# Two attention layers and a mixture of experts on one core: layer normalisations on ScalarE, their factors on GpSimd, GroupNorm's scale from PSUM, and new orders for all engines

## The reference, cut to what matters

```python
# layer 1: GroupNorm (16 groups of 4 channels), full attention, residual
h = group_norm(x, gn_scale, gn_bias, 16)
q, k, v = h@wq + bq, h@wk + bk, h@wv + bv
x = x + softmax(q k^T / 8) v @ wo + bo
# layer 2: LayerNorm over 64 channels, causal attention, residual
n = (t - mean(t)) / sqrt(var(t) + 1e-5)
t = t + softmax(mask((n Wq^T)(n Wk^T)^T / 8)) (n Wv^T)
# layer 3: LayerNorm, then 32 experts that each choose 8 tokens of an image
u = (t - mean(t)) / sqrt(var(t) + 1e-5)
probs = softmax(u gate_w^T + gate_b, over tokens)
vals, idx = top_k(probs, 8)
out = t + scatter_add(idx, vals * expert(sum(vals * u[idx])))
```

## Time and profile before

| | |
|---|---|
| median of 3 runs | 1007.56 us |
| the profiled execution: its own time | 1003.97 us |
| its span, first to last instruction | 1001.9 us |
| TensorE (PE) busy | 844.6 us, 84% |
| VectorE (DVE) busy | 718.1 us, 72% |
| ScalarE (ACT) busy | 409.4 us, 41% |
| GpSimd (POOL) busy | 348.1 us, 35% |
| granted TensorE clock, mean over the span | 0.921 |

### The profile page before, as it was taken

How to read it: one execution, slowest core, us unless ns; L and a number is a source line. 1 busy time by engine, 2 the same in 40 slices (tenths; PEclk the granted TensorE clock), 3 DMA queues, 4 the chain that set the end, 5 groups by cost and what they waited for, 6 DMA issues and landing times. The chain is left out here.

```text
span 1001.9 us, 14825 instructions
## 1 busy us (share of the span) xinstructions
PE 844.6 (84%) x4406; PEld 486.5 (49%) x4406; DVE 718.1 (72%) x1853; ACT 409.4 (41%) x792; POOL 348.1 (35%) x182
## 2 busy tenths in 40 slices
...
DMA packets 63017, 30.70 MB, mean 31 GB/s; under 512 B 35279, under 2 KB 60271, under 8 KB 62959
## 3 DMA queue, kind: packets, MB, share of 16 engines
...
...
## 5 line engine op out<-in xcount | busy, mean ns | idle before, releaser
L967 DVE TENSOR_REDUCE neg_max<-maxima_in 128x1 f32<-128x1024 f32 (+7 forms) x256 | 253.3, 990 | 106.1 <-PE maxima_in L654 93.6
L819 ACT ACTIVATE probs<-scores 128x512 f32<-128x512 f32 (+3 forms) x464 | 233.7, 538 | 163.2 <-PE scores L681 158.2
L876 POOL TENSOR_TENSOR prob_sum<-prob_sum,probs 128x1024 f32<-128x1024 f32 x96 | 227.3, 2368 | 117.3 <-ACT probs L819 112.4
L654 PE MATMUL maxima_in<-keys,queries 128*128 128x512 f32 (+3 forms) x496 | 175.2, 427 | 22.6 <-DVE neg_max L967 19.1
L681 PE MATMUL scores<-queries,keys 128*128 128x512 f32 (+3 forms) x464 | 177.0, 382 | 0.0
L696 PE MATMUL values_out<-probs,x_sb 128*64 128x512 f32 x512 | 138.1, 636 | 0.0
L654 PEld LDWEIGHTS maxima_in<-keys,queries 128*128 128x128 f32 x496 | 90.4, 207 | 88.8 <-DVE neg_max L967 58.6
L876 POOL TENSOR_TENSOR prob_sum<-probs 128x1024 f32<-128x1024 f32 x16 | 38.1, 2384 | 238.4 <-ACT probs L819 238.4
L855 POOL TENSOR_TENSOR ln<-ln,minus_half 128x8 f32<-128x8 f32 x32 | 52.7, 1648 | 192.0 <-DVE ln L1004 190.5
L679 PE MATMUL scores<-queries_lo,keys_hi 65*128 65x512 f32 x256 | 115.4, 451 | 2.3 <-DMA queries_lo<-max_rows 2.3
L681 PEld LDWEIGHTS scores<-queries,keys 128*128 128x128 f32 x464 | 91.6, 197 | 8.0
...
## 6 DMA issues: line engine op xcount, KB each, us to landing
...
```

What stands on the lines that cost most here:

```text
L654: mm = pe.matmul(maxima_in[:, lo:lo + w * P], weights, keys[s][q][:, h * HALF:h * HALF + w * P], start=not diagonal, stop=True, skip_group ...
L819: nc.scalar.activation(of(probs[:, t % NP, :]), shape(scores[:, bank_of(s, u), 0:w]), ACT.Exp, scale=SCALE).then_inc(exp_done, 1)
L876: nc.gpsimd.tensor_tensor(prob_sum[:, :], before, probs[:, t % NP, :], ALU.add).then_inc(rows_added, 1)
L967: V.tensor_reduce(neg_max[s][:, at:at + 1], maxima_in[:, HALF - widths[0] * P:HALF + widths[1] * P], AX.X, ALU.max, negate=True).then_inc( ...
```

## The change

It does four things.

1. The normalisations `l1n` and `l2n` go from VectorE to ScalarE, as factor x t + bias with factor and bias from a column each. For that, `l1p` and `l2p` on GpSimd become four operations of 128 x 8 instead of one: variance + epsilon (`ve`, before on VectorE), mean x -1 (`ng`), the power (`rs`), and -mean x factor (`nm`).
2. GroupNorm: `d` reads the group means straight from PSUM and makes difference and square in two operations that both read PSUM; `g2` averages only the square; `ab` becomes two operations on ScalarE.
3. `w_scaled` is made by a step of its own on ScalarE, `ws`, and `out1` waits for it.
4. All engines' lists are written anew. `out2`, `ri2` and `f2` come at the end of the turn before (`@-1`), `p1.tr` becomes `@+2`, at the end of a turn, and `xb` becomes `@+1`.

The core of the diff:

```diff
 ORDER = {
...
-    "pool": "ad.1 ad.2 pw@+1 ad.3 l2p@-2 ad.4 ad.5 ad.6 ad.7 xb l1p",
-    "sp": "st@-2 su@-2 row2@-1 xload@+2 row1@+1 sl@-2",
+    "pool": "l2p@-2 ad.1 ad.2 pw@+1 ad.3 ad.4 ad.5 ad.6 ad.7 xb@+1 l1p",
+    "sp": "su@-2 st@-2 sl@-2 row2@-1 xload@+2 row1@+1",
...
             elif name == "g2":
-                pe.wait_ge(gn_step, done("gn_step", n, "d2"))
-                pe.matmul(fin_ps[:, 0:2], group_mean[:, :], gn[:, 4:6], start=True, stop=True).then_inc(fin_step, 1)
+                pe.matmul(fin_ps[:, 0:1], group_mean[:, :], gn[:, 5:6], start=True, stop=True).then_inc(fin_step, 1)
...
                 if s == 1:
-                    pe.wait_ge(fin_step, done("fin_step", "w", n, "wb"))
+                    pe.wait_ge(weights_scaled, done("weights_scaled", "ws", n, "ws"))
...
+            elif name == "ab":
+                act.wait_ge(gn_step, done("gn_step", n, "pw"))
+                nc.scalar.activation(affine[q][:, 0:1], gn[:, 7:8], ACT.Identity, bias=0.0,
+                                     scale=const("gn_scale")).then_inc(gn_step, 1)
+                act.wait_ge(gn_step, done("gn_step", n, "a"))
+                nc.scalar.activation(affine[q][:, 1:2], affine[q][:, 0:1], ACT.Identity, bias=const("gn_bias"),
+                                     scale=gn[:, 2:3]).then_inc(gn_step, 1)
+            elif name == "ws":
...
+                nc.scalar.activation(w_scaled[q][:, :], w_out[1][:, :], ACT.Copy, scale=affine[q][:, 0:1]).then_inc(
+                    weights_scaled, 1)
+            elif name in ("l1n", "l2n"):
...
+                act.wait_ge(norm_step[s], done(f"norm{s}_step", n, "nm"))
+                for t in range(NT):
+                    ins = nc.scalar.activation(dst[:, t, 0:width], src[:, t, 0:width], ACT.Identity, bias=ln[s][:, 0, t:t + 1],
+                                               scale=ln[s][:, 1, t:t + 1])
+                ins.then_inc(norm_step[s], 1)
...
             elif name in ("l1p", "l2p"):
                 s = int(name[1])
+                pool.wait_ge(norm_step[s], done(f"norm{s}_step", n, "ag"))
+                nc.gpsimd.tensor_tensor(ln[s][:, 0, :], ln_mv[s][:, :, 1], eps_ln[:, :], ALU.add).then_inc(norm_step[s], 1)
+                nc.gpsimd.tensor_tensor(ln[s][:, 2, :], ln_mv[s][:, :, 0], minus_one[:, :], ALU.mult).then_inc(norm_step[s], 1)
                 pool.wait_ge(norm_step[s], done(f"norm{s}_step", n, "ve"))
                 nc.gpsimd.tensor_tensor(ln[s][:, 1, :], ln[s][:, 0, :], minus_half[:, :], ALU.pow).then_inc(norm_step[s], 1)
+                pool.wait_ge(norm_step[s], done(f"norm{s}_step", n, "rs"))
+                nc.gpsimd.tensor_tensor(ln[s][:, 0, :], ln[s][:, 2, :], ln[s][:, 1, :], ALU.mult).then_inc(norm_step[s], 1)
...
             elif name == "d":
                 dve.wait_ge(fin_step, done("fin_step", "g1", n, "mm"))
-                V.tensor_copy(gn[:, 2:4], fin_ps[:, 0:2]).then_inc(fin_step, 1)
-                dve.wait_ge(fin_step, done("fin_step", "g1", n, "gv"))
-                V.tensor_scalar(gn[:, 4:6], gn[:, 0:2], gn[:, 2:3], None, ALU.subtract).then_inc(gn_step, 1)
+                V.tensor_scalar(gn[:, 2:4], fin_ps[:, 0:2], -1.0, None, ALU.mult).then_inc(fin_step, 1)
+                V.tensor_scalar(gn[:, 4:5], fin_ps[:, 0:1], gn[:, 0:1], None, ALU.subtract).then_inc(gn_step, 1)
                 dve.wait_ge(gn_step, done("gn_step", n, "d"))
-                V.tensor_tensor(gn[:, 4:6], gn[:, 4:6], gn[:, 4:6], ALU.mult).then_inc(gn_step, 1)
+                V.scalar_tensor_tensor(out=gn[:, 5:6], in0=fin_ps[:, 0:1], scalar=gn[:, 0:1], in1=gn[:, 4:5],
+                                       op0=ALU.subtract, op1=ALU.mult).then_inc(fin_step, 1)
...
-            elif name == "ab":
...
-                V.tensor_scalar(w_scaled[q][:, :], w_out[1][:, :], affine[q][:, 0:1], None, ALU.mult)
...
-                dve.wait_ge(norm_step[s], done(f"norm{s}_step", n, "ag"))
-                V.tensor_scalar(ln[s][:, 0, :], ln_mv[s][:, :, 1], EPS_LN, None, ALU.add).then_inc(norm_step[s], 1)
-            elif name in ("l1n", "l2n"):
...
```

More of the change, by code:

```diff
@@ L91 @@
 OWN_STEPS["pe"].update({f"v{s}.{t}": (f"values_done{s}", ["v"]) for s in (1, 2) for t in range(NT)})
[L93 to L94 removed]
+IN_TURN = {"gn_step": ["ag", "d", "pw", "a", "b", "wh", "wl"],
+           "norm1_step": ["bn", "ag", "ve", "ng", "rs", "nm", "v"], "norm2_step": ["bn", "ag", "ve", "ng", "rs", "nm", "v"]}
 FIRST_TURN, LAST_TURN = -2, B + 2
@@ L345, in attention_part @@
     ln_mv = {s: sb(f"ln_mv{s}", [P, NT, 2]) for s in (1, 2)}
-    ln = {s: sb(f"ln{s}", [P, 2, NT]) for s in (1, 2)}
+    ln = {s: sb(f"ln{s}", [P, 3, NT]) for s in (1, 2)}
     x_stack = sb("x_stack", [P, S], F32R)
@@ L375, in attention_part @@
     ones_f = sb("ones_f", [P, P])
-    minus_half = sb("minus_half", [P, NT])
+    minus_half, minus_one, eps_ln = (sb(name, [P, NT]) for name in ("minus_half", "minus_one", "eps_ln"))
     group_mean = masks_f[:, 0, :]
@@ L752, in run @@
                 nc.scalar.copy(keys[2][q][0:C, HALF:S], proj_ps[C:P, :]).then_inc(proj_step, 1)
+            elif name == "ab":
[6 more added lines that the diff above has]
+            elif name == "ws":
+                act.wait_ge(gn_step, done("gn_step", n, "a"))
+                if exists(n + (-2)):
+                    act.wait_ge(fin_step, done("fin_step", "out1", n + (-2), "mm"))
+                nc.scalar.activation(w_scaled[q][:, :], w_out[1][:, :], ACT.Copy, scale=affine[q][:, 0:1]).then_inc(
+                    weights_scaled, 1)
+            elif name in ("l1n", "l2n"):
+                s = int(name[1])
+                src, dst, width = (t1[q], normed[q], C - 1) if s == 1 else (t2, u_sb, C)
+                if s == 1 and exists(n + (-2)):
+                    act.wait_ge(values_done2, done("values_done2", f"v2.{NT - 1}", n + (-2), "v"))
+                if s == 2 and exists(n + (-1)):
+                    act.wait_ge(u_stored, each(n + (-1), 16))
+                    act.wait_ge(fin_step, done("fin_step", "mtr", n + (-1), "mm"))
+                act.wait_ge(norm_step[s], done(f"norm{s}_step", n, "nm"))
[3 more added lines that the diff above has]
+                ins.then_inc(norm_step[s], 1)
             elif name == "wh":
@@ L878, in _ @@
         nc.gpsimd.memset(minus_half[:, :], -0.5)
+        nc.gpsimd.memset(minus_one[:, :], -1.0)
+        nc.gpsimd.memset(eps_ln[:, :], EPS_LN)
         nc.gpsimd.memset(ones_f[:, :], 1.0).then_inc(zeroed, 1)
@@ L922, in run @@
                 V.scalar_tensor_tensor(out=gn[:, 6:7], in0=fin_ps[:, 0:1], scalar=EPS_GN, in1=gn[:, 3:4],
[L923 to L930 removed]
+                                       op0=ALU.add, op1=ALU.subtract).then_inc(fin_step, 1)
             elif name == "wl":
```

27 lines of the change are left out of this document (3 added, 24 removed), and 38 rows, old and new, of tables (BANK_STEPS, ORDER, OWN_STEPS).

## The result

The changed kernel takes **911.87 us** (median of 4 runs, 911.33 to 912.31), the kernel before, run beside it, 1006.80: a ratio of 0.906, 95% interval 0.904 to 0.908. It is faster by 95 us.

The account below looks back on a forecast made before the run. TensorE was taken as the bound, 46.0 us of work in a 51.75 us turn. A turn of 47.0 saves 13 x 4.75 = 61.8, with the ends 69.3, giving 938 us as median; range 914 to 980.

Parts of the forecast that it names:

- the size of the turn: Per-turn time: 46.0 us of TensorE work as a floor plus 1.0 us left over, 47.0 instead of 51.75.
- small waits: Short TensorE waits expected to stay in each turn (yb, qa, the second maximum), 0.1 to 0.3 each, 1.0 us allowed.
- s1.10: Score unit needing the bank of exponential e1.7, queued behind the second normalisation on ScalarE; forecast margin -0.2 us.
- w: TensorE step needing GroupNorm's affine; a wait of some 0.2 us was to be left of 0.94.
- half speed: TensorE's clock at 1.2 instead of 2.4 GHz in stretches started by waits; 2.1 us of the old turn.
- p2.tr: TensorE step that waits for the first normalisation (normed); margin +0.4 us, so this wait was to go.
- mtr: Transposes that wait for the second normalisation (u_sb); the wait was to go, with 7 us of cover.
- the fourth rival: All margins hold and TensorE's work is a little less than read: turn below 45.3, under 916 us; chance 0.04.
- Rivals 1 and 3: 1: one wait stays, 49.5 us a turn, 971 us, chance 0.20; 3: waits only move, about 1000 us, chance 0.07.
- Rival 2: Slower: a short GpSimd operation costs what its power costs, 1.65 us; turn 57.8, 1079 us; chance 0.11.
- Start: Turns 0 and 1, where TensorE waits mostly on maxima: 3 us to be saved.
- Turn 15 and what follows: Last turn saves its 5.12 us wait and slow stretch, about 6; the last chain gets 1.5 us longer.

Follow-up runs that it names:

- moves_old_order: The changed kernel's new operations on their new engines, but in the queue orders of the kernel before; 953.20 us, ratio 0.946 to before.
- one_more_power: The changed kernel with one more 128x8 power on GpSimd in each of the two normalisation groups; 992.39 us, ratio 0.985 to before.

## Why the prediction was wrong in size and right in sign

**The step that failed is the size of the turn**: "46.0 us is TensorE's work at full clock; no order of the queues goes below it", and the 1.0 us of small waits on top of it. Measured are 45.33 us, of which TensorE is busy 45.2. The figure of 46.0 is right for the old list: moves_old_order, at a clock of 1.00, is busy 46.0 a turn. But it is not a floor. In the new list the same instructions take 0.8 us less, and 0.15 of idle time is left instead of 1.0. Nor is a busy figure work alone: the 45.2 still hold most of the 0.2 of waits at s1.10 and w. So 0.8 + 0.85 = 1.65 us of a turn were missing, 13 x 1.67 = 21.7 of the 22.2 us between the forecast difference (69.3) and that of the spans (91.5). Where in the list the 0.8 lie isn't shown: compared by operation, the issue times differ at many places by 0.1 to 0.4 us in either direction. What is left between these 91.5 and the 95 of the medians is the profiled execution of before, which lies 2.8 under the median of 1006.80, while that of after (912.31) lies 0.4 above its own median.

**The gain of a turn, put together**: 6.42 = 3.5 of idle time (3.6 less 0.15), 2.1 of half speed and 0.8 of TensorE's own time. The first two are those of the prediction.

**The margins.** Forecast -0.2 at s1.10, -0.2 at w, +0.4 at p2.tr, 7 at mtr; measured -0.18, about -0.05, +0.30, 7.5. The signs are right, at s1.10 even the size, but there by luck: from s1.0 (468.27) the exponential ends after 8.99 us instead of 9.5, and TensorE would be there after 8.86 instead of 9.3. ScalarE's side is shorter because a short GpSimd operation takes 0.20 instead of 0.35 us and the group 2.23 instead of 2.8; ScalarE's eight operations take 2.76 instead of 2.6 and give back 0.16 of that. By its time and its turn the fourth rival came, "all margins hold" with less work, under 916 us, to which I gave 0.04; its margins hold but for the 0.2 us. It needed 0.20 instead of 0.35 us for one unknown price and 0.8 us less of work in another order, and deserved more.

**The rule against the move.** The Trainium skill ("ScalarE: Activation LUTs", "Rules for kernel authors") would leave adding and multiplying on VectorE. Here the measurement decides against it: 994.02 us with u_sb on VectorE, 911.87 with it on ScalarE. Beside GpSimd's additions eight operations take 6.03 us there and 2.76 here.

**Rivals 1 and 3** did not come. **Rival 2** was right as a mechanism: with short operations at the price of the power, its 57.8 us a turn and 1079 us stand beside 58.16 and 1109.07 measured, and its deciding point of 0.73 us per operation beside one_more_power, which stands for 0.75 and is 1.5% faster than before. The turn agrees in part by luck: 45.33 + 9.1 of waits + 3.7 of half speed, where the rival had 47.0 + 7.4 + 3.4. And the price that it needed was not the real one.

**The ends.** Start: 2.4 for 3. Turn 15 and what follows: 9.9 - 4.2 = 5.7 for 6 - 1.5 = 4.5: two misses, of 3.9 and 2.7, that mostly cancel.

**Costed at nothing**, and rightly: the row DMAs, out1, xb, kB, w_lo; no wait of TensorE for any of them shows in the middle turns.
